# Macaron block on one core: the attention phase as one pipeline of 256 steps, with banks that rotate by use

## The reference

```python
def _L0_attn_ref(x, W_qkv, b_qkv, W_out, b_out):
    b, s, d = x.shape
    qkv = (x @ W_qkv.T + b_qkv).reshape(b, s, 16, 3 * 8)
    q, k, v = qkv[..., :8], qkv[..., 8:16], qkv[..., 16:]
    attn = softmax(einsum('bqhd,bkhd->bhqk', q, k) / sqrt(8))
    out = einsum('bhqk,bkhd->bqhd', attn, v).reshape(b, s, d)
    return out @ W_out.T + b_out

x = x + 0.5 * _L0_ffn_ref(_layernorm(x), ...)
x = x + _L0_attn_ref(_layernorm(x), W_qkv, b_qkv, W_out, b_out)
x = x + 0.5 * _L0_ffn_ref(_layernorm(x), ...)
```

## Time and profile before

| | us |
|---|---|
| median of three runs (1669.55 to 1698.57) | 1670.08 |
| the profiled execution | 1672.87 |
| its span | 1671.1 |
| PE busy in the span | 1572.7 (94%) |
| DVE busy | 1343.9 (80%) |
| ScalarE busy | 1208.6 (72%) |
| GpSimd busy | 957.4 (57%) |

### The profile page before, as it was taken

One profiled execution on the slowest core, in us unless ns is written; L12 is line 12 of the kernel. 1 busy time (PEld: TensorE's weight loads), 2 busy tenths in 40 slices (PEclk: granted clock), 3 DMA queues, 4 the chain that ended last, 5 costly groups with the idle time before them and its releaser, 6 DMA issues. The chain is left out here.

```text
span 1671.1 us, 26005 instructions
## 1 busy us (share of the span) xinstructions
PE 1572.7 (94%) x7309; PEld 1135.2 (68%) x7309; DVE 1343.9 (80%) x3581; ACT 1208.6 (72%) x3580; POOL 957.4 (57%) x1702
## 2 busy tenths in 40 slices
PE   4889999999999999799998988999999999999997
PEld 3667788888888887333333324788888888888884
DVE  6788889888988787578778663898899889988785
ACT  2778888888888887246556453788888888888884
POOL 3577877776777666401011001577677777776665
PEclk7999999999999999769889766999999999999999
DMA  6233533222332223000000000223332223322321
GB/s 184 81 122 127 182 137 112 101 102 101 118 129 107 102 101 126 1 1 1 1 1 1 1 1 16 111 102 128 126 108 101 102 102 127 130 104 101 108 82 51
DMA packets 42196, 147.74 MB, mean 88 GB/s; under 512 B 2500, under 2 KB 25670, under 8 KB 25670
## 3 DMA queue, kind: packets, MB, share of 16 engines
q1 hardware_dynamic: 42054, 146.09, 25.0%
HBM read 128.26 MB, written 17.83 MB: 87 GB/s over the span
## 5 line engine op out<-in xcount | busy, mean ns | idle before, releaser
L800 ACT ACTIVATE vt<-bank,gate 128x128 f32<-128x128 f32 x1024 | 292.5, 371 | 177.5 <-PE bank L362 159.4
L1119 DVE SCALAR_TENSOR_TENSOR ot<-bank,gn,ot 128x128 f32<-128x128 f32 x1024 | 288.2, 343 | 79.3 <-ACT ot L837 48.9
L1406 POOL TENSOR_TENSOR vt<-vt 128x256 f32<-128x256 f32 x256 | 194.7, 761 | 260.4 <-DVE vt L1105 260.3
L837 ACT ACTIVATE ot<-bank,gn 128x128 f32<-128x128 f32 x1024 | 291.9, 371 | 28.2 <-PE bank L362 20.9
L1105 DVE SCALAR_TENSOR_TENSOR vt<-bank,gate,vt 128x128 f32<-128x128 f32 x1024 | 285.9, 341 | 7.3 <-PE bank L362 3.9
L1429 POOL TENSOR_TENSOR ot<-ot 128x256 f32<-128x256 f32 x256 | 200.1, 782 | 83.4 <-DVE ot L1119 80.6
L1128 DVE TENSOR_TENSOR pt<-bank,pt 128x512 fp32r<-128x512 f32 x256 | 175.8, 687 | 81.2 <-ACT pt L825 80.8
L890 ACT ACTIVATE pm<-bank 128x512 f32<-128x512 f32 x256 | 144.5, 600 | 133.4 <-PE bank L603 132.3
L360 PE MATMUL bank<-wv,xhl 128*128 128x512 f32 x512 | 224.7, 439 | 15.4 <-ACT vt L800 13.6
L360 PE MATMUL bank<-wo,chl 128*128 128x512 f32 x512 | 209.0, 408 | 22.1 <-DVE chl L1088 17.7
L1249 DVE TENSOR_REDUCE mmax<-bank 128x1 f32<-128x512 f32 x256 | 165.2, 683 | 51.4 <-PE bank L584 50.4
(11 more groups left out here) (161 smaller groups left out, 3250.7 us busy)
## 6 DMA issues: line engine op xcount, KB each, us to landing
wv<-wv_split SPq DMA_DIRECT2D x56, 1024.0 KB, 4.8
wo<-wo_split SPq DMA_DIRECT2D x56, 1024.0 KB, 4.8
wv_split<-wv SPq DMA_DIRECT2D x8, 1024.0 KB, 5.1
wo_split<-wo SPq DMA_DIRECT2D x8, 1024.0 KB, 7.1
rawv<-in_L_ffn_v_w SPq DMA_DIRECT2D x8, 512.0 KB, 6.5
rawo<-in_L_ffn_o_w SPq DMA_DIRECT2D x8, 512.0 KB, 8.5
out_x<-xs SPq DMA_DIRECT2D x4, 256.0 KB, 5.7
xs<-in_L_attn_x SPq DMA_DIRECT2D x1, 768.0 KB, 8.0
```

Of the source, the lines that this page charges most:

```text
L800: last = activation(vt[:, u % 2, e * P:(e + 1) * P], gb[0][:, e * P:(e + 1) * P], ACT.Copy, scale=gate[:, n % 2, k, h * E + e:h * E + e + 1])
L837: last = activation(ot[:, u % 2, e * D:(e + 1) * D], gb[2][:, e * D:(e + 1) * D], ACT.Copy, scale=gn[:, j % 2, k, e:e + 1])
L1119: last = v.scalar_tensor_tensor(o, gb[3][:, e * D:(e + 1) * D], gn[:, j % 2, k, G + e:G + e + 1], o, ALU.mult, ALU.add)
L1406: own.link(g_.tensor_tensor(a[:, 0:2 * P], a[:, 0:2 * P], a[:, 2 * P:4 * P], ALU.add))
```

## The change

- The four batches become one pipeline: `MHA_END` steps, with `score(s)` for 256 steps and `score_t(s - LAG)` behind it; `LAG` goes from 26 to 28. No step is written per batch any more.
- Banks go by use. All that DVE or ScalarE reads at once (scores, stacks, maxima, transposes, values, products) takes the next of four banks (0, 1, 4, 5) in the order of `mha_bank_uses()`. Transposed scores rotate over three (2, 3, 6). The context has bank 7.
- `free(use)` makes PE wait for the reader of the use four places earlier.
- A stack's mask is now ScalarE's: it scales by the mask and adds the masked bias (`bsm`); DVE adds the rest. GpSimd has no part in it.
- Maxima: ScalarE copies the transposed maxima to `mt`, GpSimd adds them to the query stack.
- The value bias goes into a constant `bvb` (W_out times the bias, plus b_out), made once by two matmuls; GpSimd adds it to x (`add_constant`). The output product loses its bias matmuls, and ScalarE copies the values instead of DVE adding their bias.
- GpSimd normalises the rows of the next batch. The gates of the second FFN are spread over the last steps.
- `xT` and `vext` have two buffers, and the transposed output has its own, `oO`.

```diff
-LAG = 26
-V_STEP, PROJ_STEP = 29, 39
-TAIL = 41
+GROUPS = B * NG
+STEPS = B * MU
+LAG = 28
+MHA_END = STEPS + LAG + 17
...
+PUT_STACK, PUT_MAXIMA, TURN_OUT = (1 - GU, 3 - GU), GU + 5, GU + 5
+PUT_VALUES, TURN_NEXT, TURN_OUTPUT, PUT_OUTPUT = 12, 40, MU + 10, MU + 15
...
+        mab = [bank[0], bank[1], bank[4], bank[5]]
+        mbb = [bank[2], bank[3], bank[6]]
...
+        def mha_bank(use):
+            return mab[MHA_TURN[use] % 4]
...
+                def free(use):
+                    if MHA_TURN[use] < 4:
                         return
+                    what, i = MHA_USES[MHA_TURN[use] - 4]
+                    if what == "score":
+                        pe.wait_ge(m_max, i + 1)
+                    elif what == "stack":
+                        pe.wait_ge(qk_ready, i + 1)
...
+                def score_t(i):
...
+                    if i >= 3:
+                        pe.wait_ge(m_exp, i - 2)
                     r = slice(R * j, R * j + R)
-                    mm(bank[3 + i % 2][:], qk[r, g, 1, c * P:(c + 1) * P], qk[r, g, 0, :],
+                    mm(mbb[i % 3][:], qk[r, G % NG, 1, c * P:(c + 1) * P], qk[r, G % NG, 0, :],
...
+                for s in range(MHA_END):
                     i = s - LAG
+                    if s < STEPS:
+                        score(s)
+                    if 0 <= i < STEPS:
                         score_t(i)
+                    if i % GH == 2 and GH <= i < STEPS + GH:
                         context(i // GH - 1)
+                    for c in range(2):
+                        G = group_of(s, PUT_STACK[c])
+                        if G is not None and 1 <= G < GROUPS:
+                            stack(G, c)
+                    if group_of(s, PUT_MAXIMA) is not None:
+                        maxima(group_of(s, PUT_MAXIMA))
+                    if group_of(i, TURN_OUT) is not None:
+                        out_transposes(group_of(i, TURN_OUT))
...
+                def stack(G, c):
+                    use = ("stack", 2 * G + c)
+                    act.wait_ge(qk_mm, 2 * G + c + 1)
...
+                    activation(qk[:, g, c, :], mha_bank(use)[:], ACT.Identity, bias=bsm[:, c * NG + g:c * NG + g + 1],
+                               scale=bst[:, 2 * NG + c:2 * NG + c + 1]).then_inc(qk_high, 1)
...
+                def copy_maxima(G):
+                    act.wait_ge(m_tr, G + 1)
...
+                    activation(mt[:], mha_bank(("maxima", G))[:], ACT.Copy).then_inc(mt_copied, 1)
...
+                for s in range(MHA_END):
+                    i, b, r = s - LAG, s // MU, s % MU
+                    if s < STEPS:
+                        row_max(s)
+                    for c in range(2):
+                        G = group_of(s, PUT_STACK[c] + 2)
+                        if G is not None and 1 <= G < GROUPS:
+                            stack(G, c)
...
+                def add_maxima(G):
+                    pool.wait_ge(mt_copied, G + 1)
+                    o = qk[:, G % NG, 0, :]
+                    g_.tensor_tensor(o, o.bitcast(F32), mt[:], ALU.add).then_inc(m_added, 1)
```

More of the change, by code:

```diff
@@ L533, in ffn @@
                         context(g - 1, k)
[L535 to L543, removed]
-                        return
[L545 to L551, removed]
-                    else:
[L553 to L572, removed]
@@ L637, in output_product @@
                     for k in range(QT):
-                        o = bank[PLACE["output", 0] % 3][:, k * P:(k + 1) * P]
-                        mm(o, oT[:, k * P:(k + 1) * P], woT[:], start=True, stop=False)
-                        last = mm(o, ones[0:1, :], bout[0:1, :], start=False, stop=True)
+                        last = mm(o[:, k * P:(k + 1) * P], oO[:, k * P:(k + 1) * P], woT[:], start=True, stop=True)
                     last.then_inc(proj_mm, 1)
-                return (free, stack, value_product, score, maxima, score_t, context, out_transposes,
-                        output_transposes, output_product)
@@ L646, in mha_finish @@
[L646 to L677, removed]
-                    i = s - LAG
-                    if s == V_STEP:
-                        value_product()
-                    if s == PROJ_STEP and not first:
-                        prev[-2](lambda: free(("output", 0)))
-                    score(s)
-                    if not first:
-                        mha_finish(prev, s, False, 2 * NG * b)
-                    if i >= 0:
+                pe.wait_ge(o_fold, TILES)
@@ new lines, in mha @@
+                    if group_of(s, PUT_MAXIMA) is not None:
+                        maxima(group_of(s, PUT_MAXIMA))
+                    if group_of(i, TURN_OUT) is not None:
+                        out_transposes(group_of(i, TURN_OUT))
+                    if batch_of(s, PUT_VALUES) is not None:
+                        value_product(batch_of(s, PUT_VALUES))
+                    b = batch_of(s, TURN_NEXT)
+                    if b is not None and b < B - 1:
+                        use = ("transposes", FIRST_MHA + b + 1)
+                        free(use)
+                        prep_transpose(FIRST_MHA + b + 1, mha_bank(use))
@@ new lines, in mha @@
+                    if s == TURN_AGAIN:
+                        use = ("transposes", FIRST_AGAIN)
+                        free(use)
+                        prep_transpose(FIRST_AGAIN, mha_bank(use))
+                    if s == LOGITS_AGAIN:
+                        free(("logits", B))
+                        prep_logits(B, FIRST_AGAIN, mha_bank(("logits", B)))
+                    if batch_of(i, TURN_OUTPUT) is not None:
+                        output_transposes(batch_of(i, TURN_OUTPUT))
@@ L947, in _ @@
+            ffn(0)
+            mha()
             ffn(1)
@@ L1473, in _ @@
-            mask(0, 0)
-            for b in range(B):
-                mha_stage(b, b == B - 1)
-            pick_best(B)
+            mha()
             ffn(1)
```

544 lines of the change are left out of this document (303 added, 241 removed).

## The result

The changed kernel takes **1717.6 us**, median of four runs (1715.1 to 1734.0), beside 1671.4 for the kernel before on the same chip: a ratio of 1.028, 95% interval 1.021 to 1.036. It is slower; 1661 was forecast, with a range up to 1700. The profiled execution took 1718.9 us.

The account below looks back on a forecast made before the run. Neither engine alone bounds attention: DVE has most work, PE must feed it through three banks. Terms -0.5 (twelve groups), -3.5, -2, -1.1, -2.9, -0.7 sum to -10.7, from 1672.9 to 1662.2; forecast 1661 us, range 1620 to 1700.

Parts of the forecast that it names:

- about once a group, in 10 of the 12: Attention groups: PE's waits make the clock fall, each fall a 6.8 us half-clock stretch costing 2.2 us; 1.8 a group.
- a clock that stays low through whole groups: Attention phase: one of three signs named beforehand that would show the forecast wrong; mean clock expected 0.7 to 0.85.
- the 16.4 us of a group at full clock: Attention group of 16 steps: 8.7 plus 7.2 plus 0.5 for batch work, where before took 15.1.
- score 3 to 4: Attention group: PE waits for DVE's maximum 3 and stack, then makes the key half; 2.97 us, 1.26 of it standing.
- score 4 to 6: Attention group: PE meets the key half's bank again and waits for DVE; 2.51 us, some 0.8 standing.
- score 7 to 2 of the next group: Attention group's other stretch, 11 maxima and a split: DVE 7.0, PE 7.4, taken as 7.2 us.
- I let half of it show: Each batch's values, transposes, product, statistics and residual: some 4 us together, half counted, 0.5 a group.
- the third rival: Attention pairs on the same strips at half clock: group wholly there 26.3, half the time 21.4; 1700 us, chance 17%.
- The rule that was weighed: PE's score pairs: at lag 28 each shares its strip, so they run one behind the other, taken at 0.23 us.
- Head -2: Start of attention through groups 0 to 2: GpSimd's mask leaves the chain and a fourth bank helps; -2 us, between -5 and +2.
- Group 15 -3.5: Last attention group, without stack or wait: 15.4 us against 18.9, so -3.5.
- Tail, product and commit -4.7: End of attention: tail steps -1.1, output product with four matmuls for eight -2.9, earlier subtraction ahead of the FFN -0.7.

Follow-up runs that it names:

- The first experiment: Changed kernel, but each transposed score works on the head two further on, so on another strip than its step's score: 1676.98 us, 1.006 of before.
- lag 26 spread out, on one strip: Changed kernel with lag 26, stack halves six steps apart, transposed maxima a step earlier, transposed score on its step's score's strip: 1777.14 us.

## Why the prediction was wrong

**The step that failed** is the clock's: "about once a group, in 10 of the 12", each fall "a stretch of 6.8 us", 1.8 us a group. The falls came as forecast, nine in the twelve groups. But the stretches at half clock lasted 16 us in the mean and up to 20.5, 147 us together where 10 x 6.8 = 68 were forecast. The first of them in full, and the full clock behind it:

```profile
758.50:779.00 20.50, 17.99 (x61) 5.57 (x62) 9.98 (x18) 8.89 (x17) 1.27 (x1) 0.50 0.00 1
779.00:789.20 10.20, 7.45 (x43) 3.00 (x42) 5.28 (x10) 4.86 (x9) 0.30 (x1) 1.00 0.01 2
```

What made them long is the shared strip. The first experiment has the same banks, waits and lag and parts only the strips: its profile has eight stretches at half clock in the twelve groups, of 9 us in the mean, 72 us together. The forecast took 6.8 us from the kernel before, whose pairs are on two strips, and gave the shared strip no price at half clock, where one or two pairs take 1.15 us instead of 0.73. Its own sign of being wrong, a clock that stays low through whole groups, was there: group 2 (726.78 to 752.46) stood at half clock throughout.

**A second step was too low**, the 16.4 us of a group at full clock. Not for the price of a pair: "0.23" with the changeover of 0.42 was to be 0.65, and a pair took 0.66. The eleven pairs from score 7 to score 2, with what follows them and without a wait, took 1.41 + 0.66 + 0.66 + 1.16 = 3.9 us, where 11 x 0.23 + 3 x 0.42 = 3.8 was forecast.

The group shown above at full clock, distance by distance, forecast and then after:
- score 2 to 3: 1.63, and 1.64 (871.51 to 873.15). Right: here 0.23 + 0.42 came to the pair's 0.65.
- score 3 to 4: 2.97, and 3.00; the wait ahead of the key half 1.26, and 1.21. Right.
- score 4 to 6: 2.51, and 2.87 (876.15 to 879.02); PE stood 1.56 ahead of score 6, where some 0.8 was expected.
- score 6 to 7: 1.63, and 1.64.
- score 7 to 2 of the next group: 7.2, and 8.88 (880.66 to 889.54). PE is busy nearly all of it; 1.09 are the batch's values (884.15 to 885.24), and 0.43 a wait for ScalarE's exponential that the sum didn't have.

Together 18.0 where 16.4 was forecast. Without the values it would be 16.9, my estimate for the two groups of a batch that have neither values nor product; two groups with a product took 20.7 and 20.8 at a clock of 0.96. Two of 16.9, one of 18.0 and one of 20.7 make some 18.1 a group, rather too much, as the last holds some half clock: 12 x (18.1 - 16.4) = 20 of the missing 55 us. Mis-sized were the batch's own work, which shows with 1.1 and 3.8 us a batch where 4 x 0.5 was taken ("I let half of it show"), and some 1.0 a group in the waits. The kernel before, counted in the same way at full clock, stands at 16.1 (14.7, 15.5, 15.6 and 18.7), and lag 26 at 16.9 (15.4, 17.1, 16.6 and 18.6). A group of before at full clock, with its product, and its twelve together:

```profile
867.56:886.24 18.68, 16.91 (x97) 7.49 (x96) 14.20 (x28) 10.69 (x20) 2.08 (x2) 1.00 0.00 1
...
745.09:964.01 218.92, 200.94 (x1008) 76.18 (x1007) 164.35 (x322) 127.00 (x235) 28.44 (x30) 0.86 0.00 1
```

**The clock in us.** It makes the other 35 or more. Ten falls were to cost 21.6 us in all. A clock of 0.73 over 273 us is half clock for 54% of it, 148 us, against some 61 before (28% of 218.9, at 0.86); and 273.4 - 12 x 18.1 = 56 us is what it cost, by the estimate above. A group wholly at half clock was put at 26.3 and took 25.7 in the kernel shown above (lag 26, one strip), 27 to 32 in those with a product or a new wait. Only the third rival had this: it forecast a time of 1700 from a group of 21.4, with 17%. Its mechanism came true, strips that are shared and a clock that is low half of the time; it was itself too low, because it too took the full-clock group for 16.4. The argument against it, that PE is saturated at half clock and the clock comes back after that, was weak: in the kernel with the outputs a step earlier PE was busy 88% of the time for 220 us and the clock did not come back.

**The rule that was weighed.** The Trainium skill, page "TensorE: Matmul & The Clock Gate", Part 3, says that tiles overlap when their row groups differ, and that a weight load overlaps running matmuls only then. The trace agrees: two on one strip start 0.34 apart (871.51, 871.85), four on four strips within 0.01 us (783.37, 783.38). The prediction named it and priced it rightly at full clock; it gave it no price at half clock.

**The rest of the sum.** Head -2, measured +7.4: the clock was at half through all of groups 1 and 2, and with one strip PE set the pace there. In the first experiment, with two strips and nothing else changed, the split of group 2 was at 746.09, 1.0 later than before. Group 15 -3.5, measured -4.6. Tail, product and commit -4.7, measured -16.4: this one is larger for two reasons. The clock was full for 17 us of it, where all of it stood at half before. And the product was put at 2.9 at half clock and takes 2.05:

```profile
1068.36 2.05 PE L711 MATMUL bank<-woT,oO 128*128 128x128 f32 x8 [0.78 <-ACT oO L962]
```

Four tail steps take 2.59 us here at full clock (1048.45 to 1051.04). At half clock, in the kernel with lag 26, they take 4.03 (986.63 to 990.66) where 4.0 was forecast.

GpSimd's and ScalarE's new work costs nothing, as forecast. The residual no longer waits inside the phase: DVE stood 6.21 us ahead of it, and now comes to it without a wait.

The second FFN was to be unchanged and is 4.8 us longer. Its first 30 us ran at 0.92 in place of 0.95. That is some 2 us more at half clock, which can explain about 1 of the 4.8; the rest is open.

**What stays open** is why a shared strip holds the clock at half. In six arrangements of the stack, the maxima and the lag, one strip costs 41 to 125 us (after against its two-strip twin, and 1790.1 - 1684.4, 1788.9 - 1663.8, 1777.1 - 1679.5, 1767.8 - 1650.6, and the kernel before). Serial pairs by themselves cost 0.23 us more for one or two pairs at full clock and 0.42 at half, a few times a group; the larger part of the 125 is a clock that stays at half for up to 273 us. No count of busy time or of waits that was tried here orders the kernels by it. After itself, which has the waits at the key half, lost only 41 us to the strip, and taking those waits away lost 71 more. That it was the waits that let the clock come back is a guess, and one kernel speaks against it: lag 26 spread out, on one strip, let PE rest as long as after and had the lower clock.

## What to carry to other kernels

When a lag, an offset or a loop order changes, work out modulo the number of strips which matmuls that stand side by side now share one: here two steps of lag are 67 us, between a gain of 1.5% and a loss of 2.8%, and 41 of them are the strip alone. Price such a pair as two matmuls in a row, at both levels of the clock. Don't take the length of a half-clock stretch from a kernel whose pairs are on two strips. PE's busy share did not tell here whether the clock would come back: compare with a twin that differs in the strip alone.

## What the runs showed of the hardware

- Of two 32 x 128 matmuls over 512 columns on one strip the second starts 0.34 us behind the first at full clock, and the next full-array matmul 0.66 behind it; on two strips the next starts after 0.42. Four of them on two strips, two and two, take the same 0.66. At half clock it is 1.14 for two on one strip, 1.15 for four on two strips, and 0.73 for four on four.
- The granted clock stayed at half for 273 us in one piece in a kernel where PE's records cover 88% of the time, and stayed full over groups in which they cover 77%, with single waits up to 1.1 us.
- With the same banks, waits and lag, twelve groups had eight stretches at half clock of 9 us in the mean on two strips, and nine of 16 us on one.
- GpSimd's addition of 128 x 512 took 1.27 us where its operands were the stack and the copied maxima, and 1.04 in the operation of the earlier trace rows.
